# A macaron block on one Trainium2 core: a reordered first stage, three token groups ahead of the expert slots and four behind them, five row buffers, and TensorE's operands at multiples of 512 bytes

## The reference

```
x = x + 0.5 * ffn(layernorm(x))
x = x + ssm(layernorm(x))
x = x + 0.5 * ffn(layernorm(x))

def swiglu(x, wg, wu, wd): return silu(x @ wg.T) * (x @ wu.T) @ wd.T
def ffn(x):
    logits = x @ gate_w.T                     # 8 experts
    top_id, score = argmax(logits), sigmoid(max(logits))
    shared = swiglu(x, shared_gate, shared_up, shared_down)        # F = 512
    routed = sum over e of swiglu(where(top_id == e, x * score, 0), r_gate[e], r_up[e], r_down[e])
    return shared + routed
def ssm(x):    # W_in (256 to 512), causal convolution of 4 taps, a 16-state recursion, silu, W_out
```

## Time and profile before

| | |
|---|---|
| median of 3 runs | 888.17 us (885.1 to 893.15) |
| the profiled execution's own time | 891.24 us |
| its span in the profile | 889.4 us |
| PE busy | 843.3 us, 95% of the span |
| DVE, ACT, POOL busy | 480.9, 382.1, 460.8 us |
| DMA | 128.66 MB, mean 145 GB/s |

### The profile page before, as it was taken

The page is one execution under the profiler, slowest core; times in us unless marked ns, Lnnn a source line. Parts: engine busy times, 40 slices in busy tenths (PEclk is TensorE's granted clock), DMA queues, the critical chain, the costliest instruction groups (busy, mean ns, idle before and its releaser), DMA issues.

```text
span 889.4 us, 16359 instructions
## 1 busy us (share of the span) xinstructions
PE 843.3 (95%) x5398; PEld 734.9 (83%) x5399; DVE 480.9 (54%) x1012; ACT 382.1 (43%) x749; POOL 460.8 (52%) x427
## 2 busy tenths in 40 slices
PE   3999989999999999998998999999999999999993
PEld 2788878888888888887887988988888888888883
DVE  6987553333333335668998885856333333333452
ACT  3353223333333333456776776333243443434230
POOL 5627670333333008869999983477331233330685
PEclk9999999999999999997999999999999999999997
DMA  9795663445555316222011016457445555521566
GB/s 309 259 327 172 204 221 109 159 163 197 189 199 191 101 50 114 40 42 30 17 45 31 24 45 223 123 189 244 167 132 189 200 189 201 177 70 35 107 150 153
DMA packets 72695, 128.66 MB, mean 145 GB/s; under 512 B 6746, under 2 KB 64228, under 8 KB 68292
## 3 DMA queue, kind: packets, MB, share of 16 engines
q0 software_dynamic: 17536, 74.33, 26.9%
q1 hardware_dynamic: 54610, 53.63, 19.1%
q10 hardware_dynamic: 498, 0.02, 0.0%
HBM read 91.64 MB, written 36.32 MB: 144 GB/s over the span
## 4 chain that ended last, share of the span: by engine, by line
PE 61%; POOL 15%; DVE 8%; DMA 7%; issue 5%; ACT 2%; ACTq 0%; POOLq 0%; SPq 0%; DVEq 0%
PE bank L383 18%; PE bank L384 17%; PE bank L385 17%; POOL acc L1792 5%; PE bank L591 4%; POOL xs_sorted L1725 3%; DMA rows<-xn_kept 2%; DVE v L1429 2%; DMA xs_sorted<-rows,pos 2%; DMA wr_hi<-w_routed 2%; PE bank L560 2%; POOL v L1697 2%; PE bank L450 2%; POOL wr_lo L1765 1%; POOL yr L1901 1%
## 5 line engine op out<-in xcount | busy, mean ns | idle before, releaser
L1765 POOL TENSOR_TENSOR wr_lo<-wr_raw,wr_hi 128x3072 fp32r<-128x3072 f32 x14 | 95.3, 6807 | 95.9 <-DMA wr_hi<-w_routed 92.1
L383 PE MATMUL bank<-wr_hi,xT_hi 128*128 x312 | 130.2, 417 | 1.6 <-POOL wr_lo L1765 1.5
L384 PE MATMUL bank<-wr_hi,xT_lo 128*128 x312 | 123.8, 397 | 0.0
L385 PE MATMUL bank<-wr_lo,xT_hi 128*128 x312 | 122.9, 394 | 0.0
L1134 DVE TENSOR_TENSOR hT_lo<-bank,hT_hi 128x512 fp32r<-128x512 f32 x78 | 53.9, 692 | 124.8 <-ACT hT_hi L843 124.8
L1387 DVE TENSOR_TENSOR hf<-sg,bank 128x512 f32<-128x512 f32 x78 | 53.7, 689 | 125.1 <-PE bank L385 125.1
L1792 POOL DMA_INDIRECT acc<-ys_sorted,pos x52 | 86.6, 1664 | 54.2 <-DMA ys_sorted<-rows 39.8
L383 PE MATMUL bank<-xT_hi,ws_hi 128*128 128x512 f32 x256 | 102.2, 399 | 0.4 <-DVE ws_lo L1551 0.4
L384 PE MATMUL bank<-xT_hi,ws_lo 128*128 128x512 f32 x256 | 100.6, 393 | 0.0
L385 PE MATMUL bank<-xT_lo,ws_hi 128*128 128x512 f32 x256 | 100.5, 393 | 0.0
L843 ACT ACTIVATE xT_hi<-bank 128x256 fp32r<-128x256 f32 (+1 forms) x126 | 56.0, 464 | 99.8 <-PE bank L560 88.8
(11 more groups left out here) (234 smaller groups left out, 2115.1 us busy)
## 6 DMA issues: line engine op xcount, KB each, us to landing
wr_raw<-w_routed POOLq DMA_DIRECT2D x16, 1536.0 KB
wr_hi<-w_routed POOLq DMA_DIRECT2D x16, 1536.0 KB
rows<-xs_sorted SPq DMA_DIRECT2D x78, 128.0 KB, 2.6
ys_sorted<-rows SPq DMA_DIRECT2D x78, 128.0 KB, 1.7
xn_kept<-xg SPq DMA_DIRECT2D x16, 512.0 KB, 3.6
rows<-xn_kept SPq DMA_DIRECT2D x16, 512.0 KB
xg<-xn_kept SPq DMA_DIRECT2D x12, 512.0 KB
acc<-x SPq DMA_DIRECT2D x8, 512.0 KB, 9.9
```

The lines of the kernel that those rows point to most:

```text
L383: pe.matmul(o, a_hi, b_hi, start=start, stop=False, skip_group_check=True)
L384: pe.matmul(o, a_lo, b_hi, start=False, stop=False, skip_group_check=True)
L385: return pe.matmul(o, a_hi, b_lo, start=False, stop=stop, skip_group_check=True)
L1765: pool.tensor_tensor(wr_lo[:, e % 2, :], wr_raw[:, :], f32(wr_hi[:, e % 2, :]), ALU.subtract).then_inc(s_wl, 1)
```

## The change

It does five things.

1. **First stage.** `norm_apply` of groups 1, 3, 4 and 5 moves from DVE to ACT, with two more small POOL steps each for the shift; gate and up weights are rounded and cut in two halves; the hand-written order on PE, ACT and DVE is another; the stores of zeros to `xs_sorted` go out behind the 7th and the 8th `rsqrt` in place of the 4th to 8th.
2. **Order around the slots.** Three groups ahead of the slots, four behind, in both feed-forward steps. In L = 0, 28 gathers go out ahead of the state-space loop and group 3's last four in its steps n = 0 to 3.
3. **Rows.** Five buffers (`ROW_RING`): three more in the space of the second expert's `wr_lo`. The load of group g waits for the scatter of group g - 5, so that the first five are loaded ahead. `cut_expert(L, 1)` now waits until the scatters from these three have landed.
4. **Routing.** The steps from the sums over tiles to `pos` are shared: POOL does two while DVE goes on, DVE does the last four; the three `cut_part` go from POOL to DVE.
5. **Addresses.** Pads of 384 and 96 bytes, and tensors moved, so that all tensors that TensorE reads in the long stages begin at a multiple of 512 bytes.

```diff
-        def half_groups(L, half): return ORDER[L][1:NH + 1] if half == 0 else ORDER[L][NH + 1:]
+        def half_groups(L, half): return ORDER[L][1:NH] if half == 0 else ORDER[L][NH:]
...
+        sb("lead_pad", [P, 96], F32)
...
+        sb("over_pad", [P, 24], F32)
...
+        spare = ExitStack()
+        sb("spare_pad", [P, 4 * W], F32, spare)
+        more_rows = sb("more_rows", [P, 3 * GT, H], F32, spare)
+        spare.close()
...
+        def row_buffer(g):
+            b = g % ROW_RING
+            return rows[:, b * GT:(b + 1) * GT, :] if b < 2 else more_rows[:, (b - 2) * GT:(b - 1) * GT, :]
+
+        def row_uses(L, g): return L * len(range(g % ROW_RING, NG, ROW_RING)) + g // ROW_RING
...
+        ON_ACT = (1, 3, 4, 5)
+        ON_DVE = (0, 2, 6, 7)
...
-        LATE = half_groups(1, 1)
-        ADDED = [{}, {3: (LATE[0],)}, {2: (LATE[1],), FB: (LATE[2],)}]
-
-        GATHERED = (6, 7, LATE[0], 0, LATE[1], 1, LATE[2], 2)
+        LATE = half_groups(1, 1)[2:]
+        ADDED = [{}, {}, {}, {1: (LATE[0],), FB: (LATE[1],)}]
+
+        GATHERED = (6, 7, 0, 1, 2, LATE[0], 3, LATE[1])
...
             r1_transposes(0)
-            setup_ssm(2)
-            setup_ssm(3)
-            r1_logits(0)
-            setup_ssm(4)
-            r1_transposes(1)
             pe.wait_ge(s_wsl, 1)
             shared_gu(0, 0, 0)
+            r1_logits(0)
+            setup_ssm(2)
+            r1_transposes(1)
+            shared_gu(0, 0, 1)
+            r1_logits(1)
+            r1_transposes(2)
...
+            def norm_apply(g):
+                act.wait_ge(s_nb1, ON_ACT.index(g) + 1)
+                if g >= 2:
+                    act.wait_ge(s_xt, 2 * (t_r1(g - 2) + 1))
+                    act.wait_ge(s_xc[g % 2], 16 * (g // 2))
+                for t in range(GT):
+                    ins = act.activation(xg[:, g % 2, t, :], acc[:, g * GT + t, :], ACT.Identity,
+                                         bias=shift[:, g % 4, t:t + 1], scale=rstd[:, g % 4, t:t + 1])
+                ins.then_inc(s_xna, 1)
...
-                dve.tensor_scalar(ne[:, 2, :], before, float(P), None, ALU.mult).then_inc(s_cum, 1)
+                chained(dve.tensor_scalar(ne[:, 2, :], before, float(P), None, ALU.mult))
                 dve.tensor_copy(after_e[:, :], src[0:1, :])
+                t3 = pfx[:, 0, :, :]
+                dve.wait_ge(s_rank, L + 1)
+                chained(dve.tensor_tensor(t3, t3, ne[:, 2:3, :].to_broadcast([P, NT, E]), ALU.add))
+                chained(dve.tensor_tensor(t3, t3, oh[:, :, :], ALU.mult))
+                chained(dve.tensor_reduce(m2[:, :], t3, AX.X, ALU.add))
+                dve.tensor_copy(pos[:, :], m2[:, :]).then_inc(s_pos, 1)
...
-            SCALED = ([{3: (0,), FB: (1,)}, {1: (2,), 3: (3,)}, {0: (4,), 2: (5,), FB: (6,)}, {1: (7,)}],
-                      [{1: (0,), 2: (1,)}, {1: (2,), 3: (3,)}, {0: (4,), 2: (5,), FB: (6,)}, {1: (7,)}])
+            SCALED = ([{2: (0,), 3: (1,), FB: (2,)}, {0: (3,), 1: (4,), 3: (5,)}, {0: (6,), 1: (7,)}],
+                      [{1: (0,), 2: (1,), 3: (2,), FB: (3,)}, {0: (4,), 2: (5,), FB: (6,)}, {1: (7,)}])
+
+            CUT = {(1, FB): 0, (2, 0): 1, (2, 2): 2}
...
+            def cut_part(L, i):
+
+                if i == 0:
+                    dve.wait_ge(s_wraw, 16 * (L * E + 1))
+                    dve.wait_ge(s_wh, 16 * (L * E + 1))
+                ws = slice(i * W // 3, (i + 1) * W // 3)
+                ins = dve.tensor_tensor(wr_lo[:, 0, ws], wr_raw[:, ws], f32(wr_hi[:, 0, ws]), ALU.subtract)
+                if i == 2:
+                    ins.then_inc(s_wl, 1)
...
+            def r1_rsqrt(g):
+                p = g % 4
+                rsqrt(k_r1(g), p)
+                if g in ON_ACT:
+                    a = ON_ACT.index(g)
+                    pool.wait_ge(s_rs, k_r1(g) + 1)
+                    pool.tensor_tensor(ve[:, p, :], mv[:, p, :, 0:1].squeeze(2), rstd[:, p, :],
+                                       ALU.mult).then_inc(s_nb1a, 1)
+                    pool.wait_ge(s_nb1a, a + 1)
+                    pool.tensor_scalar(shift[:, p, :], ve[:, p, :], -1.0, 0.0, ALU.mult, ALU.add).then_inc(s_nb1, 1)
...
+            def token_ranks(L):
 
                 pool.wait_ge(s_cum, L + 1)
                 t3 = pfx[:, 0, :, :]
                 row_step(pool.tensor_tensor(t3, t3, cum[:, 0, :, :], ALU.add))
+                pool.tensor_tensor(t3, t3, pfx[:, 1, :, :], ALU.subtract).then_inc(s_rank, 1)
...
-            for g in range(NG):
-                rsqrt(k_r1(g), g % 4)
-                if g >= NG - ZERO_STORES:
-                    s0 = (g - NG + ZERO_STORES) * 2 * GT
-                    c = min(2 * GT, NS - s0)
-                    pool.dma_start(xs_slot[:, s0:s0 + c, :], rows[:, 0:c, :]).then_inc(s_zero, 16)
+            for g in range(NG - 1):
+                r1_rsqrt(g)
+            for i in range(ZERO_STORES - 1):
+                zero_slots(i)
+            r1_rsqrt(NG - 1)
+            zero_slots(ZERO_STORES - 1)
...
             def load_rows(L, g):
...
-                if n >= 2:
-                    sp.wait_ge(s_sct[g % 2], 64 * (n // 2))
-                sp.dma_start(rows[:, g % 2 * GT:(g % 2 + 1) * GT, :], tiles(xn, g)).then_inc(s_rl[g % 2], 16)
+                if L == 0 and g == 0:
+                    sp.wait_ge(s_zero, 16 * ZERO_STORES)
+                if L == 0 and g == 2:
+                    sp.wait_ge(s_wsl, 3)
+                if L == 1 and g == 2:
+                    sp.wait_ge(s_vb, 4 * NG)
+                if g >= ROW_RING:
+                    sp.wait_ge(s_sct[g % ROW_RING], 64 * row_uses(L, g))
+                sp.dma_start(row_buffer(g), tiles(xn, g)).then_inc(s_rl[g % ROW_RING], 16)
...
+                for g in range(NG - ROW_RING, NG):
+                    if g % ROW_RING >= 2:
+                        pool.wait_ge(s_sct[g % ROW_RING], 64 * (row_uses(L, g) + 1))
                 cut_expert(L, 1)
...
-                if 1 <= n <= GT:
-                    gather_tile(NG - 1, n - 1, s_ga[NG - 1])
+                if n < GT:
+                    if n == 0:
+                        pool.wait_ge(s_add, 2 * NG)
+                    gather_tile(NH - 1, n, s_ga[NH - 1])
...
-                if n == 0:
-                    pool.wait_ge(s_add, 2 * NG)
-                    gather(3, s_ga[3])
```

More of the change, by code:

```diff
@@ L266, in build @@
         s_scl = sem("rows_scaled")
-        s_rl = [sem("rows_loaded_even"), sem("rows_loaded_odd")]
-        s_sct = [sem("scattered_even"), sem("scattered_odd")]
+        s_rl = [sem(f"rows_loaded{b}") for b in range(ROW_RING)]
+        s_sct = [sem(f"scattered{b}") for b in range(ROW_RING)]
         s_tab = sem("slot_table_done")
@@ L295, in build @@
         s_ga = [sem(f"gathered{g}") for g in range(NG)]
-        s_fin = [sem(f"last_gathered{g}") for g in range(NG)]
         s_fad = sem("gathered_rows_added")
@@ L335, in f32, with ws_part @@
             return ap.bitcast(F32)
+        def ws_part(buf, part, pair):
+            if part == 1:
+                return buf[:, DN0:W]
+            half = F // 2
+            return buf[:, 0:DN0].rearrange("p (a f) -> p a f", f=F)[:, :, pair * half:(pair + 1) * half]
         def tiles(buf, g, n=GT):
@@ L773, in r1_transposes @@
             def r1_transposes(g):
-                transposes(g % 2, s_xn, g + 1, min(g, 1), f_r1(g))
+                ready_sem, ready = xn_ready(g)
+                transposes(g % 2, ready_sem, ready, min(g, 1), f_r1(g))
             def r1_logits(g):
@@ L815, in _ @@
             r1_logits(4)
+            r1_transposes(5)
+            setup_ssm(7)
+            setup_ssm(8)
+            r1_logits(5)
+            r1_transposes(6)
+            setup_ssm(9)
             setup_ssm(10)
-            r1_transposes(5)
-            pe.wait_ge(s_wsl, 2)
+            r1_logits(6)
+            r1_transposes(7)
+            pe.wait_ge(s_wsl, 3)
             pe.wait_ge(s_setv, 12)
@@ L878, in shared_group @@
                         hi(qq[:, :], QF[:, :]).then_inc(s_fla, 1)
-                    if L == 0 and half == 0 and fb == 2 and i == 3:
+                    if L == 0 and half == 0 and fb == 2 and i == 2:
                         act.wait_ge(s_tzp, 1)
@@ L1299, in shared_group @@
                         dve.wait_ge(s_hl, 4 * n + fb - 1)
-                    if L == 0 and half == 1 and i == 1 and 1 <= fb <= 2:
+                    if L == 0 and half == 1 and i == 2 and 1 <= fb <= 2:
                         ln2_stats(fb - 1)
@@ L1315, in shared_group @@
                         setup_rows_lo()
-                    if L == 0 and half == 0 and fb == 3 and i == 3:
+                    if L == 0 and half == 0 and fb == 3 and i == 2:
                         setup_toeplitz_lo()
+                    if L == 0 and half == 0 and fb == 1 and i == 1:
+                        setup_b_out()
                     if fb > 0:
@@ L1923, in routed_slots @@
             def routed_slots(L):
-                for a in range(2):
```

(21 more changed lines are left out.)

238 lines of the change are left out of this document (116 added, 122 removed).

## The result

The changed kernel takes 905.98 us (median of 4 runs, 904.27 to 907.61) where the kernel before takes 886.64 (4 runs, 885.10 to 893.15): ratio 1.0186, 95% interval 1.0151 to 1.0222. It is slower by 1.9%, and the time lies above the predicted range. The recorded execution has a span of 905.3 us where that of before has 889.4.

What follows compares the result with a forecast made beforehand. PE was taken as the bound, busy 843.3 of 889.4 us. Terms -0.4 + 0 - 1.5 + 3.7 + 1 - 4.8 - 3 = -5.0 us gave 886.2 on the profiled execution, 883 on the median; range 856 to 894.

Steps and rivals of the forecast that it cites:

- the row of scatters: Ahead of the slots: with five buffers and no cuts on POOL, 32 scatters go without a stop in 40.3 us.
- -0.4: Ahead of L = 0's slots: one group (17.54 us) moves behind them, last scatter issued 17.9 us earlier; net -0.4 us.
- 3.7 + 1: Ahead of L = 1's slots: last scatter 13.85 us earlier where 17.54 were wanted, +3.7; +1 for a lower clock.
- the scatters start late and set both slot starts: Slower rival: zero stores land late, first scatter 3 us later, PE stands in both layers; 898 us, chance 0.16.
- 69 was the alarm: Sign ahead of L = 0's slots: forecast wrong above all if POOL starts its first scatter later than 69.
- State-space step: Step after L = 0's slots: fewer gathers ahead of the biases on POOL, stop for `xT_lo` stays; -1.5 us.
- the state-space step is freed: Rival: the stop and the low clock there both go, -6 us in place of -1.5; 878 us, chance 0.08.
- The end: Kernel's end: gathers are done early, so the last store follows DVE's additions, same 6.1 us behind it; -4.8 us.
- The addresses: PE's matmuls: all operands lie as in the shared part, slot spacing becomes 0.227 and 0.120 us; -3 us.
- the rival of a free run (857): Rival: aligned operands let long matmuls run at 0.213 and 0.107 us, priced at half, 29 us; 857, chance 0.20.
- the one that the addresses do nothing: Rival: matmul spacings stay at 0.235 and 0.117 us in the slots, all else as forecast; 886 us, chance 0.13.
- The first stage: Start of kernel: PE ends it 1 to 3 us earlier, but slot 0 waits for scatters; counted 0.

Runs made afterwards that it cites:

- e9: The changed kernel, unchanged, run again as control on another chip: 888.52 us.
- e10: The changed kernel without the pads, operands where they lay before, on the same chip as e9: 5.1 us above e9.
- e2: The changed kernel with only the addresses undone (no pads, three tiles back in their old places): 892 us.
- e7: The changed kernel without pads, expert 1's raw weights loaded behind the rows of the first three slots: 899.13 us.
- e8: The changed kernel without pads, expert 1's raw weights loaded ahead of the last four scatters: 908.91 us.
- e3: The kernel before with nothing but the pads and moved tiles: nine executions from 880.8 to 891.9 us, one of 2127.3.
- series 2 and 5: Series 2: the changed kernel (905.85 us), e6, e7 and e8 on one chip; series 5: e17 and e18 on another.
- series 1, 3 and 4: Variants beside the kernel before, one chip per series; the unchanged changed kernel, absent from the first, took 888.52 and 887.69 us in the other two.
- e17: The changed kernel with 3 us POOL memset stops behind scatter groups 1, 3 and 5 in L = 0 only: slot 0 of L = 0 at 127.91 us.
- e18: The changed kernel with two small POOL memsets behind each scatter in L = 0 only: slot 0 of L = 0 at 134.75 us.
- e6: The changed kernel with the first pad 256 bytes shorter: equal in time to the unchanged changed kernel on its chip, 905.85 us.

## Why the prediction was wrong, step by step

**The step that failed is the row of scatters.** "32 of them go in a row", taken as pure gain (40.3 us from first to last), was costed by what one scatter takes, and its effect on others was put at nothing. They took 51.5 us in L = 0 and 52.4 in L = 1, because the unbroken row held back PE's completions, DVE's scaling came late behind them, and the scatters waited for it. Of the 18.8 us by which e9 and the first result differ in the terms ahead of the slots (-0.4 became +13.6 and not +3.8, 3.7 + 1 became +19.7 and not +10.6), 16.7 are this; the other 2.1 are the lower clock of the first stage. The trace of before held a hint that was not looked for: the `silu` that was 1.5 us late at the end of a row of eight. No rival named this; the slower one ("the scatters start late and set both slot starts") had another cause, and it fell: the first scatter came at 67.67, where 67.3 was forecast and 69 was the alarm.

**Scatters on a chip without lateness** (e9): from 65.5, 1.8 earlier than forecast, to a last issue at 108.7, so 43.1 us where 40.3 were taken; several took 1.3 to 2.0 us. So even here the term was too small. Slot 0 then came 8.85 us behind the last issue, where 5.75 was carried over from before. That term missed what the change moved: `load_raw(L, 1)`, in front of the last four scatters before, is now right behind them, ahead of the slot's rows. Net +3.8 us in L = 0, where -0.4 was said.

**L = 1:** +10.6 where +3.7 and +1 were said (e9), by three things: the start not earlier (8.3 us behind the gate of the table, 8.0 before), the row 44.2 us long, and 8.1 from the last issue to slot 0. With the late completions it was +19.7.

**State-space step:** -1.5 was taken from the near end of 0 to -6; measured -7.1 and, in e9, -6.3. The step itself went from 149.9 to 142.8 us. The wait for `xT_lo` stayed at 2.9 us as forecast, but PE's idle time fell from 7.65 to 4.2 us in all, and its busy time from 142.2 to 138.6: the lower level of the clock lasted 3.4 us where it had lasted 10.2. The rival "the state-space step is freed" was right in size, though the stop did not go.

**The end:** -4.8 forecast, -10.2 measured. The last store does follow DVE's last addition:

```profile
898.19 1.22 DVE L1412 TENSOR_TENSOR acc<-acc,yr 128x1024 f32<-128x1024 f32 x1
...
902.15 0.69 DVE L1342 SCALAR_TENSOR_TENSOR acc<-bank,acc 128x512 f32<-128x512 f32 x1 [1.40 <-PE bank L416]
```

From the end of that addition to the end of the span it is 2.5 us, where the earlier trace rows gave 10.9. I had kept the 6.1 us behind the last store as if they were the store's. They weren't: in the trace of before SP is through with the last store at 886.2, and what ends at 889.2, just ahead of the span's end, is POOL's closing DRAIN, an entry of its sequencer that is open from 860.6 on. In the view of that line, before and then after (duration in ns, start in us):

```profile
L72 POOLq DRAIN  x1: 28637/28637/28637, 860.6 to 860.6; - x1
L73 POOLq DRAIN  x1: 28203/28203/28203, 872.5 to 872.5; - x1
```

It ends 8.3 us behind the end of POOL's last gather before (880.90) and 8.8 behind it after (891.90), and between 8.0 and 8.8 in every trace of the study. With the gathers done early it ends at 900.7, ahead of the last store, and the store alone sets the end.

**The addresses:** the spacing came out as forecast. PE's timeline in a slot, six matmuls of 512 columns apart, then nine of 256:

```profile
151.73 0.39 PE L416 MATMUL bank<-wr_lo,xT_hi 128*128 x1
...
153.09 0.39 PE L416 MATMUL bank<-wr_lo,xT_hi 128*128 x1
...
153.78 0.28 PE L416 MATMUL bank<-wr_lo,hT_hi 128*128 x1
...
154.86 0.28 PE L416 MATMUL bank<-wr_lo,hT_hi 128*128 x1
```

0.227 and 0.120, the shared part's figures, as in the earlier trace rows. Between e9 and e10 the slots of both layers differ by 1.2 + 0.8 = 2.0 us, for the -3 that was said; the rival of a free run (857) is out, the one that the addresses do nothing is out for the slots. In time e10 stands 5.1 us above e9. Another 2.7 lie ahead of slot 0 of L = 0: all four traces of the new order without pads (e2, e7, e8, e10) have the clock at the lower level for 3.4 us near 28, none with pads has; why, was not tried. On the kernel before (e3) the pads can't be told from nothing in time: ten executions, nine from 880.8 to 891.9 us and one of 2127.3. Its trace has the slots 3.2 us shorter than that of before (185.9 and 183.9), near the -3, but that is one execution on another chip.

**The first stage:** 0 forecast, and the prefix came at 55.70, before 56.00. That is luck: in e9 it comes at 53.56, 2.4 us earlier than before, and the first scatter at 65.53. The new order gained the 1 to 3 us that were expected of it, this moved `choose` and the prefix after all, and in the first result the lower clock took them back.

So without the late completions and the lower clock the sum would have been off by 2 us only (e9's span is 2.9 below that of before, 5.0 were forecast), and that by luck, for the errors cancel: +4.2 and +5.9 ahead of the slots, +2.2 in the slots, -4.8 and -5.4 in the state-space step and at the end. The kernel is a draw there: 0.9975 and 0.9987.

## What to carry to other kernels

Taking the stops out of a queue of indirect DMAs is not free for the other engines: look in the trace of before at the distance from a matmul's end to its consumer's start near the end of the longest row, and treat any growth there as a warning. When a step is moved, list every DMA that it issues and what it now stands in front of; one bulk load of 1.5 MB moved behind the scatters cost 7 us, more than the whole forecast gain. A cure is worth only what it gives on the path that sets the time: the stops ended the lateness and cost as much. And a difference of 2% between two kernels can belong to the chip or the moment: before blaming an edit, run the changed kernel itself beside its variants.

## What the runs showed of the hardware

PE's completions can reach ACT and DVE up to 15.8 us late while POOL issues indirect DMAs every 1.27 us, from the sixth to tenth on: in the first result and in series 2 and 5, and not in series 1, 3 and 4; the five series ran on five chips. The 2.83 us pause ended it, and at the 1.7 us pace it did not arise (e17 and e18). The distance between matmuls of 512 and 256 columns depends on how their operands lie to each other, and not on multiples of 512: 0.228 and 0.120 us where they lie alike, also when all are moved by 256 bytes together (e6), and 0.234 and 0.117 where they lie 96 bytes apart (e10).
